# A transformer block on one core: expert lists by counting, and FFN weights split once and kept in device memory

## What is computed

```python
x = x + _L0_xattn_ref(_layernorm(x), ctx_512, ctx_512, ...)   # 16 heads, causal
x = x + _L0_ffn_ref(_layernorm(x), ...)    # dense FFN of width 1376, with low-rank experts
x = x + _L1_xattn_ref(_layernorm(x), ctx_512, ...)
x = x + _L1_ffn_ref(_layernorm(x), ...)    # 64 experts, 8 for a token, width 192
```

```python
pos = (jnp.cumsum(onehot, axis=0) * onehot).sum(-1) - 1
valid = pos < CAP
dest = jnp.where(valid, slot_expert * CAP + pos, E * CAP)
```

## Time and profile before

| what | value |
|---|---|
| median of 3 runs | 1466.43 us (1465.83 to 1467.62) |
| the profiled execution | 1466.93 us |
| its span | 1465.1 us |
| instructions | 19951 |
| busy: PE / PEld / DVE / ACT / POOL | 1219.6 / 892.1 / 826.5 / 498.4 / 488.2 us |
| moved by DMA | 180.77 MB, mean 123 GB/s |

### The profile page before, as it was taken

The page is one execution under the profiler, slowest core; times in us unless marked ns, Lnnn a source line. Parts: engine busy times, 40 slices in busy tenths (PEclk is TensorE's granted clock), DMA queues, the critical chain, the costliest instruction groups (busy, mean ns, idle before and its releaser), DMA issues. The chain is left out here.

```text
span 1465.1 us, 19951 instructions
## 1 busy us (share of the span) xinstructions
PE 1219.6 (83%) x6297; PEld 892.1 (61%) x6297; DVE 826.5 (56%) x1677; ACT 498.4 (34%) x1137; POOL 488.2 (33%) x539
## 2 busy tenths in 40 slices
PE   0698999887899987789998788998406999999990
PEld 0566777655777765567786566776204666666660
DVE  7674777576677758577866846664582222222220
ACT  1582312565222167422127633221202323333230
POOL 3530222633022372302236230121004555555541
PEclk9998999998999999999999989999757999999995
DMA  7002221000322100042200003220078999999966
GB/s 254 1 1 93 79 97 60 1 1 30 121 84 103 52 1 1 30 135 95 97 34 0 1 32 114 103 104 0 29 318 261 349 355 342 340 358 349 292 89 130
DMA packets 44659, 180.77 MB, mean 123 GB/s; under 512 B 5356, under 2 KB 8428, under 8 KB 35764
## 3 DMA queue, kind: packets, MB, share of 16 engines
q1 hardware_dynamic: 29732, 140.15, 25.5%
q0 software_dynamic: 14864, 39.85, 12.0%
HBM read 149.28 MB, written 34.90 MB: 126 GB/s over the span
## 5 line engine op out<-in xcount | busy, mean ns | idle before, releaser
L1819 PE MATMUL PS<-WE,XGT 128*128 128x384 f32 x512 | 194.8, 504 | 1.5 <-DVE HM L1929 0.8
L682 ACT ACTIVATE P<-PS,NM 128x512 f32<-128x512 f32 (+3 forms) x256 | 132.2, 536 | 50.7 <-DVE NM L1054 49.6
L1367 PE MATMUL PS<-XTH,WHI 128*128 128x512 f32 x352 | 141.6, 402 | 1.3 <-ACT SIL L825 1.3
L811 ACT ACTIVATE WHI<-WRAW 128x1280 fp32r<-128x1280 f32 x44 | 56.1, 1274 | 248.9 <-DMA WRAW<-in_ffn 248.9
L1368 PE MATMUL PS<-XTL,WHI 128*128 128x512 f32 x352 | 139.9, 397 | 0.0
L1369 PE MATMUL PS<-XTH,WLO 128*128 128x512 f32 x352 | 139.6, 397 | 0.0
L596 POOL CAST HH<-HID 128x512 fp32r<-128x512 f32 x44 | 28.1, 639 | 328.6 <-DVE HID L1279 317.1
L1232 DVE TENSOR_TENSOR WLO<-WRAW,WHI 128x584 fp32r<-128x584 f32 (+1 forms) x88 | 110.8, 1259 | 29.4 <-ACT WHI L811 17.3
L1054 DVE TENSOR_REDUCE NM<-PS 128x2 f32<-128x1024 f32 (+2 forms) x96 | 98.7, 1042 | 48.2 <-PE PS L1376 47.6
L1819 PEld LDWEIGHTS PS<-WE,XGT 128*128 128x128 f32 x512 | 88.2, 192 | 57.9 <-issue 23.5
L1427 PE MATMUL PS<-ident,P 128*128 128x128 f32 x640 | 101.6, 297 | 23.1 <-ACT P L682 12.8
(11 more groups left out here) (273 smaller groups left out, 2768.1 us busy)
## 6 DMA issues: line engine op xcount, KB each, us to landing
WE<-in_we SPq DMA_DIRECT2D x64, 1152.0 KB, 8.2
WRAW<-in_ffn SPq DMA_DIRECT2D x44, 932.0 KB, 4.6
hx<-HN SPq DMA_DIRECT2D x4, 1152.0 KB, 4.4
acc<-HN SPq DMA_DIRECT2D x17, 256.0 KB, 4.6
XIN<-in_x SPq DMA_DIRECT2D x4, 1024.0 KB, 10.5
out<-X SPq DMA_DIRECT2D x4, 1024.0 KB, 4.2
out<-acc POOLq DMA_DIRECT2D x1, 4096.0 KB, 23.0
CTX<-in_ctx SPq DMA_DIRECT2D x4, 256.0 KB, 7.5
```

The costliest lines, as they stand in the source:

```text
L682: act.activation(prob(t, n), PS[:, c0:c0 + (t + 1) * P], ACT.Exp, bias=NM[:, c:c + 1], accum_out=SSUM[:, c:c + 1]).then_inc(S["p_ready"], 1)
L811: act.activation(WHI[slot][:, 0:WD], WRAW[slot][:, 0:WD], ACT.Copy).then_inc(S["wg_hi"], 1)
L1367: pe.matmul(dst, a[0], b_[0], start=first, stop=False, **kw)
L1819: mm = pe.matmul(bank(2 + s % 2, 0, 2 * F1), XGT[s % 2][:, k, :], WE[s][:, k * 2 * F1:(k + 1) * 2 * F1], start=(k == 0), stop=(k == KC - 1))
```

## The change

**The split weights.** `WHI` and `WLO` of a slot become the two halves of one tile `WHL` (14,912 bytes in each partition). In batch 0 the weights are loaded and split as before; SP then stores each finished pair to a new tensor `split` in device memory, and ACT waits for the store of chunk f - 2 before it writes into that slot again. In batches 1 to 3 there is no splitting: SP loads the pair of halves, 1864 KB, straight into `WHL`. `WHL` has two buffers. The products are the same.

**The lists.** A token's place in its expert's list is counted: PE multiplies the masks with a triangle of ones (`before`) and with ones, which gives the number of earlier tokens of each expert; `TAKEN` carries the count over the batches. The place is cut into a high part (16 values) and a low part (8 values), DVE writes both as rows of zeros and ones in bf16, and PE multiplies them for 8 experts at a time, which puts each token's number at its place. The result is kept in `SLOTS`. In batches 1 to 3 these steps for the batch before stand between the chunks of the FFN (`list_step`); those of the last batch stand alone (`last_list`). `KEYS`, `revt`, `list_round` and the 16 rounds at the start of part 3 are gone.

**Part 3** is in the same block as the rest now. SP loads 6 experts' weights during the last FFN, behind the loads of chunks 2 to 7, and 6 more right behind that FFN. The loops over chunks are written out.

The core of the diff (tiles that only move, and code of part 3 that is only renamed, are left out):

```diff
-    WHI = [sb(f"WHI{s}", [P, WCOLS], F32R) for s in range(2)]
-    WLO = [sb(f"WLO{s}", [P, WCOLS], F32R) for s in range(2)]
+    WHL = [sb(f"WHL{s}", [P, 2 * WCOLS], F32R) for s in range(2)]
+    WHI, WLO = [t[:, 0:WCOLS] for t in WHL], [t[:, WCOLS:2 * WCOLS] for t in WHL]
...
+            def load_split(f):
+                sp.dma_start(WHL[f % 2][:, :].bitcast(F32), split[span(f, P), :]).then_inc(w_loaded[f % 2], 16)
+
+            def store_split(f):
+                sp.dma_start(split[span(f, P), :], WHL[f % 2][:, :].bitcast(F32)).then_inc(split_stored, 16)
...
+                    sp.wait_ge(split_stored, 16 * NF)
+                    load_split(0)
+                    load_split(1)
...
-                with sp.Fori(1, NF // 2) as i:
-                    load_w(2 * i, 0)
-                    load_w(2 * i + 1, 1)
-                load_w(NF - 1, 0)
+                for f in range(2, NF):
+                    if b == 0:
+                        halves_made(f - 2)
+                        sp.dma_start(WRAW[f % 2][:, :], w["ffn"][span(f, P), :]).then_inc(w_loaded[f % 2], 16)
+                        store_split(f - 2)
+                    else:
+                        sp.wait_ge(S["dn_ps"], 1 + b * NF + f - 1)
+                        alone(sp, "sp")
+                        load_split(f)
+                    if last and f < 8:
+                        load_expert(f - 2, f - 2)
...
+                def wg_hi(f, slot):
+
+                    act.wait_ge(w_loaded[slot], 16 * (f // 2 + 1))
+                    if f > 1:
+                        act.wait_ge(split_stored, 16 * (f - 1))
...
-                w_rest(0, 0, 0, WD, "wg_hi", "wg_lo")
-                if b > 0:
+                if b == 0:
+                    w_rest(0, 0, 0, WD, "wg_hi", "wg_lo")
+                else:
                     dve.wait_ge(S["lgt_ps"], 1 + b)
...
+                step(dve.tensor_scalar(AT[:, :, :], SR[:, :, :], 0.0, FAR, ALU.is_ge, ALU.mult))
+                if b > 0:
+                    step(dve.tensor_tensor(AT[:, :, :], AT[:, :, :], TAKEN[:, :].unsqueeze(1).broadcast_to([P, NT, E1]),
+                                           ALU.add))
...
+            def positions(b, bk):
+
+                pe.wait_ge(S["mk_ready"], 1 + b + 1)
+                for t in range(NT):
+                    for u in range(t + 1):
+                        mm = pe.matmul(bank(bk, t * E1, (t + 1) * E1), (before if u == t else ones)[:, :], MK[:, u, :],
+                                       start=(u == 0), stop=(u == t))
...
                 def gate_up(f, slot, parts="weights lora"):
                     hi, lo = WHI[slot], WLO[slot]
-                    pe.wait_ge(S["wg_lo"], 1 + b * NF + f + 1)
+                    if b == 0:
+                        pe.wait_ge(S["wg_lo"], 1 + f + 1)
+                    else:
+                        pe.wait_ge(w_loaded[slot], 16 * (b * SLOT_LOADS[slot] + f // 2 + 1))
...
-                with pe.Fori(0, NF // 2) as i:
-                    for d in (1, 2):
-                        gate_up(2 * i + d, d % 2)
-                        down(2 * i + d - 1, (d + 1) % 2)
+                for f in range(NF - 1):
+                    gate_up(f + 1, (f + 1) % 2)
+                    down(f, f % 2)
+                    if b > 0:
+                        list_step(b - 1, f)
...
-            for c in range(CAP // 8):
-                src, dst, group = KEYS[c % 2], KEYS[1 - c % 2], LST[:, 8 * c:8 * c + 8]
-                step(dve.max(group, src[:, :]))
-                step(dve.match_replace(dst[:, :], group, src[:, :], -1.0))
```

More of the change, by code:

```diff
@@ L110, in build @@
     zrow = sb("zrow", [1, 512], BF16)
[L111 to L115, removed]
     mhalf = sb("mhalf", [P, 8])
     IDX = sb("IDX", [P, E1], U32)
-    part3_base = place["at"]
+    before = sb("before", [P, P], BF16)
+    ones = sb("ones", [P, P], BF16)
+    steps_of = sb("steps_of", [P, SA + SB])
+    numbers = sb("numbers", [P, 3])
+    same = sb("same", [P, GE])
+    SLOTS = sb("SLOTS", [P, C])
+    TAKEN = sb("TAKEN", [P, E1])
+    AT = sb("AT", [P, NT, E1])
+    MK = sb("MK", [P, NT, E1], BF16)
+    lists_base = place["at"]
+    HIGH = [sb(f"HIGH{i}", [P, E1, SA], BF16) for i in range(2)]
+    tables_base = place["at"]
     cosw = sb("cosw", [P, NT, C])
@@ L273, in build @@
     acc_zeroed, combined = sem("acc_zeroed"), sem("combined")
+    lists_loaded, spread_loaded, idx_ready = sem("lists_loaded"), sem("spread_loaded"), sem("idx_ready")
+    expert_loaded = [sem(f"expert_loaded{s}") for s in range(NW)]
+    gathered = [sem(f"gathered{s}") for s in range(NX)]
+    LISTS = [(before, w["before"]), (ones, w["ones"]), (steps_of, w["steps_of"]), (numbers, w["numbers"]),
+             (same, w["same"])]
     tables_loaded, setup_loaded, setup_dve, setup_act, tables_made = (sem(n) for n in (
@@ L416, in ring, with experts, call @@
                     *(turned_by(ALONE, by) - turned_by(BESIDE, by) + turned_by(BESIDE, by) * a for by in "ad"))
+    def experts(engine, body, start, stop):
+        rounds = (stop - start) // NW
+        def call(i, d):
+            body((i * NW + start + d), (start + d) % NW, i + (start + d) // NW)
+        with engine.Fori(0, rounds) as i:
+            for d in range(NW):
+                call(i, d)
+        for e in range(start + rounds * NW, stop):
+            body(e, e % NW, e // NW)
     with nc.Block() as block:
@@ L615, in two_chunks @@
                         front_q(b + 1, i)
-                two_chunks(0)
-                alone(pool, "pool")
-                with pool.Fori(1, NF // 2 - 1) as i:
+                for i in range(NF // 2 - 1):
                     two_chunks(i)
@@ new lines, in expert @@
+            def expert(e, s, r):
+                pool.wait_ge(M["hm"], 1 + e + AHEAD - NX + 1)
+                gather(e + AHEAD, (s + AHEAD) % NX)
+                scatter(e, s, r)
+            pool.wait_ge(S["hx_stored"], 16 * (B + 2))
+            pool.wait_ge(idx_ready, 1)
+            for e in range(AHEAD):
+                gather(e, e)
+            pool.wait_ge(S["out_stored"], 16 * (B + 1))
+            pool.wait_ge(acc_zeroed, 16 * (ROWS // P))
+            for e in range(NX - AHEAD):
+                gather(e + AHEAD, e + AHEAD)
+                scatter(e, e, 0)
@@ new lines, in _ @@
+            alone(pool, "pool")
+            experts(pool, expert, NX - AHEAD, E1 - AHEAD)
+            for e in range(E1 - AHEAD, E1):
+                scatter(e, e % NX, e // NX)
+            for parity in range(2):
+                pool.wait_ge(scattered[parity], 16 * (E1 // 2))
+            pool.dma_start(out[0:NTOK, :].rearrange("(a f) c -> a (f c)", f=NT),
+                           acc[0:NTOK, :].rearrange("(a f) c -> a (f c)", f=NT),
+                           accum_op=ALU.add, max_dma_last_dim=8192).then_inc(combined, 16)
@@ L1303, in two_chunks @@
                             front_q(b + 1, i)
[L1304 to L1306 removed]
+                for i in range(NF // 2 - 1):
                     two_chunks(i)
                 chunk(NF - 2, 1)
+                if b > 0:
+                    list_step(b - 1, NF - 2)
                 if not last:
@@ new lines, in one_hots, with clear @@
+            def one_hots(bk, high, low, last):
+                for e in range(0, E1, GE):
+                    mm = pe.matmul(bank(bk, e * SB, (e + GE) * SB), high[:, e:e + GE, :].rearrange("p e a -> p (e a)"),
+                                   low[:, e:e + GE, :].rearrange("p e c -> p (e c)"), start=False, stop=last,
+                                   skip_group_check=True)
+                return mm
+            def clear(bk):
+                pe.matmul(bank(bk), zrow[:, 0:P], zrow[:, :], start=True, stop=False, skip_group_check=True)
```

584 lines of the change are left out of this document (320 added, 264 removed).

## The result

The changed kernel takes 1761.87 us (median of 4 runs, 1757.52 to 1765.7) against 1466.13 us (median of 4, 1463.35 to 1467.62): a ratio of 1.199, 95% interval 1.192 to 1.205. The profiled execution took 1765.7 us, with a span of 1763.9 us.

What follows compares the result with a forecast made beforehand. The dense FFN was taken as bound by TensorE alone, with the lists on the path behind batch 3. 1466.9 + 263 + 26 - 5 - 20 = 1731 us, range 1695 to 1775, slower with chance 0.98.

Steps and rivals of the forecast that it cites:

- 27 stalls: FFN chunks 2 to 10, batches 1 to 3: TensorE waits 7.5 us per pair load, plus 2.25 for the clock; +263 us.
- The clock's part: Behind each TensorE wait in batches 1 to 3: work at half clock after the restart loses 2.25 us.
- at the rate of long traffic: Rival: transfers run at 350 GB/s, each wait 0.7 us longer and 11 us more in batch 0; 1761 us, chance 0.10.
- The list steps: List products on TensorE between FFN chunks fit into the waits: cost 0; without that cover, 7 us a batch.
- Batch 0: Batch 0's FFN: load, added store and splitting make a chunk 13.3 us against 10.46, 9 times; +26 us, ends 17 and 37.
- Start of the FFN: Ahead of the gates in batches 1 to 3: less DVE work and no mask turning, 1.7 us a batch; -5 us.
- The lists: Behind batch 3, last mask to indices: 17.2 us in place of 37.2; -20 us, ends -14 and -24.
- The signs: Profile after: 27 `WHL<-split` waits near 7 us, batch 3's FFN stretch half idle, clock near 0.85, chunks 20.2 and 13.3 us.

Runs made afterwards that it cites:

- waits filled: The changed kernel with 28 products of a zero matrix in front of each of the 27 waits for a pair; 1705.34 us, ratio 1.164.
- half store: The changed kernel, batches 1 to 3 loading only each pair's high half and batch 0 storing only that half; 1647.88 us, ratio 1.120.
- kernel with pieces: The changed kernel with each pair loaded in two pieces, gate and up columns after the up products, down columns after the down products; 1498.06 us, ratio 1.022.
- half load: The changed kernel with batches 1 to 3 loading only the high half of each pair, 932 KB in place of 1864; 1665.62 us, ratio 1.138.
- the lists alone: The counted lists without stored pairs: weights are split in every batch as in the kernel before; 1464.93 us, ratio 1.000 to the kernel before.

## Why the prediction was right

The forecast was 1731 us, from 1695 to 1775, slower; the result is 1762. The mechanism is the predicted one. The miss of some 31 us is mostly batch 0. The sizes of the terms against what was measured:

- **27 stalls, +263 us.** The chunks of batches 1 to 3 take 269.3 us more than before, 9.97 each against 9.75. From the end of `down(0)` to the restart it is 7.9 us in the rows above (805.14 to 813.00), where the forecast had 7.2 and 0.3 for the refill: landing takes 7.4 us, not 6.8, and the list products fill the first 0.6 of it. The clock's part is 2.1 us by the run with the waits filled (2.25). So the sum is near, with the transfer too low and the clock a little too high. The load has another make-up than I gave it: 2.0 us fixed and 353 GB/s, not 2.35 and 425. The rival "at the rate of long traffic" was right about the rate, but too dear by 13 us for the stalls and too cheap by 10 for batch 0; that its 1761 us are the result is chance.
- **The list steps, 0.** They are free only under the stalls. Where the stalls are gone they cost 2.9 us a batch, less than half of the 7 that I named for that case.
- **Batch 0, +26 us.** This step failed. It was mis-sized: 47 us in the profile after, of which 41.4 are in the chunks; 39 to 43 there in the other runs that store whole pairs. "Load and store together ... 6.7 us at 425 GB/s, and 2.7" made 9.4 us from the halves to ACT's next start; it took 11.3 (DVE's halves end at 177.66, ACT starts at 188.92). A load and a store at once moved their 2.86 MB at 334 GB/s if 2.7 us are fixed. My upper end, 37 us at 350 GB/s, was too low as well (its own terms, 8.2, 2.7 and 3.9, make 14.8 us a chunk, and 39). The half store, which took 23.8 us off, shows that it is bytes. Of the other 5.6 us of 47, 5.5 lie ahead of the first chunk and are the clock of one execution, below.
- **Start of the FFN, -5 us.** Nothing came of it: 108.8 us over three batches against 108.5. `LG` did come 3.2 us earlier in all, but from there to the first product of `down(0)` it took 3.6 us longer. The granted clock of batches 2 and 3 in this stretch was 0.81 and 0.82, against 0.90 before. The clock was not in my term; what sets it there stays open. In the kernel with pieces the start gained 1.4.
- **The lists, -20 us.** Measured -19.7, and the path 17.35 us against 17.2.
- **The signs.** `WHL<-split` 27 times at 7.3 us; the stretch two thirds busy at 0.80, where I said half idle and 0.85 (a wait of 7.5 in a period of 20.2 would be little over a third). Landing 7.4, not 6.8, and the clock back in 4.8, not 4.5: wrong in size by my own sign, right in kind. A chunk in batches 1 to 3 took 20.4 us against 20.2, in batch 0 14.9 against 13.3.

The differences of the profiled executions are 269.3 (chunks), 41.4 and 5.5 (batch 0), 0.3 (start), -19.7 (lists) and 1.9 for the rest. With 1466.9 they make 1765.6, and the profiled execution took 1765.7. They are stretches of one trace, so they have to add up; the experiments, not this sum, show the causes.

The Trainium skill (TensorE: Matmul & The Clock Gate, HAM oscillation — how this bites in real kernels) finds 1.67 us at the low clock behind each of its kernel's DMA waits; half of it, 0.8 us, would be the work lost, an estimate. The rows disagree: 4.8 us at the low clock on the mean behind waits of 7.3 us, 3.3 behind waits of 4.6, and 2.1 us of work lost by the run with the waits filled. The Trainium skill's page on transfers (DMA: Bandwidth & Descriptors, Where 436 GB/s comes from) has 358 GB/s for the memory side. The 353 of the half load agree with it, the 383 over 35 us of the earlier trace rows don't.

## What to carry to other kernels

Work on engines that have room beside the bound one was free here, and a transfer that replaces it has to find a free buffer a whole turn ahead; ask first which product last reads the tile that the load writes. Where a buffer can't be spared, load it in the pieces in which it comes free: here that was worth 264 us with the same bytes and tiles. A small product that costs nothing inside a wait costs its time once the wait is gone. And a wait of TensorE cost more here than its length, so when a gain doesn't arrive, compare stretch by stretch, the chunks and the stretch ahead of them apart: here the lists' 20 us were lost again in both.

## What the runs showed of the hardware

The clock's return is not a constant. In batch 0 of the profiled execution after the change TensorE worked for 16 us without a gap at half clock; in a run with the same code for batch 0 it was back after 5 us of the same products. The kernel after, then the run with the waits filled:

```profile
134.50:151.50 17.00, 16.09 (x70) 15.61 (x71) 7.82 (x24) 3.75 (x6) 0.20 (x1) 0.50 0.43 165
151.50:156.00 4.50, 4.50 (x22) 3.59 (x22) 2.41 (x11) 0.00 (x0) 0.00 (x0) 1.00 0.00 0
```

```profile
135.50:140.00 4.50, 4.50 (x22) 4.50 (x23) 3.48 (x7) 2.73 (x5) 0.00 (x0) 0.50 1.02 382
140.00:151.00 11.00, 11.00 (x72) 9.88 (x72) 6.01 (x27) 1.02 (x2) 0.00 (x0) 0.98 0.14 55
```

It was seen in one of the nine profiled executions; in the others the low stretch there lasted 7 us in all. What decides it stays open. Second, behind a wait of 4 us, with light work on its other side, the clock was at 0.55 for 15 us (the lists alone, 907 to 922), where it came back 4.0 to 5.6 us after the waits of 7.3 us between dense products. Third, loads of 932 and 1864 KB that ran alone fit 353 GB/s behind 2.0 us, though a stretch of 2 us before the change showed 438.
